# Routing block of an attention and mixture-of-experts kernel: parts of the down products ahead of two waits, and the second early batch's addition moved into the expert block

## What is computed

```python
logits = (x @ wt.T + repeat(g @ wg.T)) / 2
topk_w, topk_idx = top_k(softmax(logits), 2)      # weights normalised to sum 1
y_all = einsum('etm,emh->eth', leaky(x @ w_gate) * (x @ w_up), w_down)
y = (y_all[topk_idx] * topk_w).sum(1)
p = (leaky(x @ sw_gate) * (x @ sw_up)) @ sw_down  # the shared expert
out = x + y + p
```

## Time and profile before

| What | us |
|---|---|
| median of three runs (lowest, highest) | 1751.0 (1750.06, 1754.42) |
| the profiled execution, device time | 1752.34 |
| its span, first to last instruction | 1750.6 |
| PE busy / PEld busy | 1622.9 / 1357.3 |
| DVE / ACT / POOL busy | 972.0 / 719.0 / 730.9 |
| routing block: PE's first matmul to the first of the expert block | 1057.77 to 1158.86 |
| mean granted TensorE clock | 0.969 |

### The profile page before, as it was taken

The page is one execution under the profiler, slowest core; times in us unless marked ns, Lnnn a source line. Parts: engine busy times, 40 slices in busy tenths (PEclk is TensorE's granted clock), DMA queues, the critical chain, the costliest instruction groups (busy, mean ns, idle before and its releaser), DMA issues. The chain is left out here.

```text
span 1750.6 us, 36162 instructions
## 1 busy us (share of the span) xinstructions
PE 1622.9 (93%) x10364; PEld 1357.3 (78%) x10365; DVE 972.0 (56%) x2442; ACT 719.0 (41%) x1823; POOL 730.9 (42%) x1177
## 2 busy tenths in 40 slices
PE   6899987999999999996999997989999999899998
PEld 4777766887888888885888886768777788678886
DVE  5444525776677766775655555624333333356565
ACT  3222325776776766775222221114333343312221
POOL 1000234676676676674655550332222222234222
PEclk9999997999999999998999998989999999999999
DMA  6576657776776766876544452043455533246333
GB/s 214 202 243 227 221 197 219 210 221 187 215 208 187 209 196 180 233 198 160 171 152 159 144 174 78 1 186 108 174 223 216 208 108 106 85 128 221 97 103 114
DMA packets 172361, 301.32 MB, mean 172 GB/s; under 512 B 16658, under 2 KB 64322, under 8 KB 170196
## 3 DMA queue, kind: packets, MB, share of 16 engines
q1 hardware_dynamic: 142324, 235.21, 42.1%
q0 software_dynamic: 11200, 35.73, 7.2%
q10 hardware_dynamic: 18720, 29.12, 4.9%
HBM read 186.99 MB, written 113.00 MB: 171 GB/s over the span
## 5 line engine op out<-in xcount | busy, mean ns | idle before, releaser
L754 POOL TENSOR_SCALAR probs<-probs,rsums 128x512 f32<-128x512 f32 (+3 forms) x512 | 265.1, 536 | 198.6 <-DVE rsums L790 198.5
L782 DVE CUSTOM_DVE_ANT_0 scores<-psum,resident 128x514 f32<-128x514 f32 (+3 forms) x512 | 242.6, 484 | 156.9 <-PE psum L897 136.9
L855 ACT ACTIVATE probs<-scores,lowest 128x514 f32<-128x514 f32 (+3 forms) x512 | 284.3, 557 | 35.0 <-DVE lowest L782 33.8
L909 PE MATMUL psum<-ident,probs 128*128 128x128 f32 x1280 | 234.3, 282 | 19.1 <-DVE probsT L797 13.2
L897 PE MATMUL psum<-keys,queries 128*128 (+4 forms) x640 | 221.2, 354 | 24.0 <-DMA queries_and_ones<-q_hi_d 17.3
L909 PEld LDWEIGHTS psum<-ident,probs 128*128 128x128 f32 x1280 | 150.6, 141 | 53.6 <-issue 39.9
L897 PE MATMUL psum<-keys_lo_and_mask,queries_and_ones 128*128 (+4 forms) x640 | 184.5, 297 | 0.0
L929 PE MATMUL psum<-probsT,v_now 128*64 128x128 f32 x2560 | 169.5, 279 | 0.9 <-DVE probsT L797 0.9
L897 PEld LDWEIGHTS psum<-keys,queries 128*128 128x128 f32 x640 | 126.9, 198 | 34.9 <-issue 20.6
L929 PEld LDWEIGHTS psum<-probsT,v_now 128*64 128x64 f32 x2560 | 138.6, 138 | 14.6 <-issue 1.9
L864 ACT ACTIVATE probsT<-psum 128x512 f32<-128x512 f32 (+2 forms) x192 | 93.6, 488 | 134.5 <-PE psum L909 121.2
(11 more groups left out here) (240 smaller groups left out, 3689.6 us busy)
## 6 DMA issues: line engine op xcount, KB each, us to landing
ys_d<-y_out ACTq DMA_DIRECT2D x71, 256.0 KB
q_hi_d<-q_hi SPq DMA_DIRECT2D x64, 256.0 KB, 2.4
q_lo_d<-q_lo SPq DMA_DIRECT2D x64, 256.0 KB, 2.8
queries<-q_hi_d SPq DMA_DIRECT2D x64, 256.0 KB, 3.7
queries<-q_lo_d SPq DMA_DIRECT2D x64, 256.0 KB, 4.1
queries_and_ones<-q_hi_d SPq DMA_DIRECT2D x64, 256.0 KB, 4.5
oT_d<-o_out SPq DMA_DIRECT2D x64, 256.0 KB, 2.3
o_in<-oT_d SPq DMA_DIRECT2D x32, 512.0 KB, 3.9
```

The lines of the kernel that those rows point to most:

```text
L754: pool.tensor_scalar(out=row, in0=row, scalar1=rsums[:, n % RING:n % RING + 1], scalar2=1.0, op0=ALU.mult, op1=ALU.mult).then_inc(probs_sc ...
L782: dve.tensor_tensor_reduce(out=scores[n % 4][:, 0:CK[i]], in0=score_psum(n), in1=bias_of(resident, i, h), scale=1.0, scalar=3.0e38, op0=AL ...
L855: act.activation(probs[n % RING][:, 0:CK[i]], scores[n % 4][:, 0:CK[i]], ACT.Exp, bias=lowest[:, n % 4:n % 4 + 1], scale=-1.0, accum_out=s ...
L909: last = pe.transpose(probsT_bank[g % 2][:, at + j * P:at + (j + 1) * P], probs[n % RING][:, AHEAD + j * P:AHEAD + (j + 1) * P], ident[:])
```

## The change

`down` gets the chunks that it shall do, and the four `down` of a batch are split in two. `begin_down(b)` waits for the third chunk's `h_lo` and does chunks 0 to 2 of token tiles 0 and 1; `end_down(b)` waits for the fourth, does its three matmuls for both tiles, and then tiles 2 and 3 whole. For batch 0 the one stands right behind the other; for batch 1 `find_tokens(6)` and `find_tokens(7)` stand between them. The additions of x1 to batch 1's tiles leave the routing block: POOL makes two behind the gather of expert tile 2 and two behind that of tile 3, and SP waits for all eight additions before it loads x1 of batch 2 over the buffers.

```diff
+def add_x(pool, partial, x1, b, t, x_added):
+    pool.tensor_tensor(out=partial[:, TB * b + t, :], in0=partial[:, TB * b + t, :], in1=x1[b][:, t, :], op=ALU.add
+                       ).then_inc(x_added, 1)
...
             for t in range(TB):
-                add_x(0, t)
+                pool.wait_ge(y_copied, t + 1)
+                add_x(pool, partial, x1, 0, t, x_added)
...
                 gather_rows(pool, dram, route, ident, spare, s, s, rows, xg, rows_ready, xg_loaded)
-            for t in range(TB):
-                add_x(1, t)
...
-            def down(b, t):
-                if TB * b + t >= 2:
+            def down(b, t, js):
+                if js[0] == 0 and TB * b + t >= 2:
                     pe.wait_ge(y_copied, TB * b + t - 1)
...
-                for j in range(SC):
+                for j in js:
...
-                done.then_inc(y_full, 1)
+                if js[-1] == SC - 1:
+                    done.then_inc(y_full, 1)
+
+            def begin_down(b):
+
+                pe.wait_ge(h_lo_ready, SC * b + SC - 1)
+                for t in range(2):
+                    down(b, t, range(SC - 1))
+
+            def end_down(b):
+                pe.wait_ge(h_lo_ready, SC * b + SC)
+                for t in range(2):
+                    down(b, t, range(SC - 1, SC))
+                for t in range(2, TB):
+                    down(b, t, range(SC))
...
-            pe.wait_ge(h_lo_ready, SC)
-            for t in range(TB):
-                down(0, t)
+            begin_down(0)
+            end_down(0)
...
+            begin_down(1)
             find_tokens(6)
             find_tokens(7)
-            pe.wait_ge(h_lo_ready, 2 * SC)
-            for t in range(TB):
-                down(1, t)
+            end_down(1)
...
                     gather_rows(pool, dram, route, ident, spare, s, k, rows, xg, rows_ready, xg_loaded)
+                    if known(s) and s < 4:
+
+                        for t in range(2 * (s - 2), 2 * (s - 1)):
+                            add_x(pool, partial, x1, 1, t, x_added)
...
+            sp.wait_ge(x_added, EARLY_B * TB)
             for b in range(EARLY_B, EARLY_B + 2):
                 load_x1(sp, dram, x1, b, b % 2, x1_loaded)
```

More of the change, by code:

```diff
@@ L124, in build @@
             xg_loaded = [held.enter_context(nc.semaphore(f"xg_loaded{i}")) for i in range(2)]
+            x_added = held.enter_context(nc.semaphore("x_added"))
             stage_route(nc, dram, psum, ident, logits, shared, route, experts, experts_loaded, x1, x1_loaded, partial,
-                        spare, rows, xg, rows_ready, xg_loaded)
+                        spare, rows, xg, rows_ready, xg_loaded, x_added)
             stage_experts(nc, dram, psum, ident, spare, experts, experts_loaded, route, x1, x1_loaded, rows, xg,
-                          rows_ready, xg_loaded)
+                          rows_ready, xg_loaded, partial, x_added)
         stage_shared(nc, dram, psum, ident, spare, shared, route, x1, x1_loaded, partial, out)
@@ L1240, in stage_route @@
 def stage_route(nc, dram, psum, ident, logits, shared, route, experts, experts_loaded, x1, x1_loaded, partial, spare, rows,
-                xg, rows_ready, xg_loaded):
+                xg, rows_ready, xg_loaded, x_added):
     with ExitStack() as ctx:
@@ L1284, in stage_route @@
                                                     sem("y4_copied"))
-        tokens_ready, x_added = sem("tokens_ready"), sem("x4_added")
+        tokens_ready = sem("tokens_ready")
         at = 2 * EW
@@ L1337, in tile_hots @@
                                    op=ALU.mult).then_inc(tile_hot_ready, 1)
-            def add_x(b, t):
-                pool.wait_ge(y_copied, TB * b + t + 1)
-                pool.tensor_tensor(out=partial[:, TB * b + t, :], in0=partial[:, TB * b + t, :], in1=x1[b][:, t, :], op=ALU.add
-                                   ).then_inc(x_added, 1)
             for t in range(TB):
-                add_x(0, t)
+                pool.wait_ge(y_copied, t + 1)
+                add_x(pool, partial, x1, 0, t, x_added)
             for g in range(GROUPS):
@@ L1624, in _ @@
                     find_tokens(2 * j - 1)
+            begin_down(1)
             find_tokens(6)
             find_tokens(7)
-            pe.wait_ge(h_lo_ready, 2 * SC)
-            for t in range(TB):
-                down(1, t)
+            end_down(1)
 def stage_experts(nc, dram, psum, ident, spare, experts, experts_loaded, route, x1, x1_loaded, rows, xg, rows_ready,
-                  xg_loaded):
+                  xg_loaded, partial, x_added):
     with ExitStack() as ctx:
```

## The result

The changed kernel takes **1739.97 us**, the median of ten runs (1732.28 to 1747.44), against 1751.45 (1743.16 to 1757.08) for ten runs of the kernel before beside it: a ratio of 0.9928, 95% interval 0.9909 to 0.9946, or 12.6 us less by the ratio (9.5 to 15.9). The profiled execution has a span of 1734.8 against 1750.6.

The account below looks back on a forecast made before the run. PE, busy for 93% of the span, was taken to bound the kernel. Batch 0's 5.4 and batch 1's 7.9 sum to 13.3 us off, other terms 0: 1739.0 for the profiled execution, median 1737.7, range 1735.5 to 1743.5.

Parts of the forecast that it names:

- Batch 0: Routing block: 18 matmuls fill PE's wait for `h_lo`, the half clock behind it goes, a bank wait costs 0.2; 5.4 us gained.
- Batch 1's tail: Routing block's end: 18 matmuls fill the 3.42 idle ahead of group 6 and the half clock ends; part of 7.9 us.
- The clock: Batch 1, behind thin matmuls and 0.7 us idle in two pieces: full clock holds, 0 lost; bound 2.4 if it falls.
- the row that held: Profile row of PE where 1.71 us of thin matmuls stood between wide ones and the wide ones kept full steps.
- The first rival: Half clock stays at batch 1: 12 matmuls take 5.26 instead of 2.83, gain 10.9, time 1740.1; chance 0.16.
- Barrier and additions: Routing block's end: ACT's last copy replaces POOL's last addition as the end; leaving the barrier costs 0.52; part of 7.9.
- The moved additions: POOL, expert block: four additions of 1.26 hide behind its waits of 3.67 and 2.50 for PE; cost 0, bound 0.7.
- The bound of 2.5: Expert block's first gathers lose cover; at the slowest gather's 10.7 us they would land 2.5 too late; 0 taken.
- DVE and POOL as the new bound: Rival: DVE and POOL set the pace in the routing block, batch 0's gain is lost, 7.9 left, 1743.1; chance 0.08.
- The slower rival: Expert block: additions hold up gathers, PE waits, never made up; 1756.3 and over; chance 0.04.
- the formula: Slower rival's sum: loss is the four additions' time beyond the pairs' cover of 3.67 and 2.50, 6.2 in all.
- the break-even: Slower rival's threshold: each addition would have to take 6.2 us, losing 18.6, to be slower by over 5.3.

Follow-up runs that it names:

- The first split alone: Against the changed kernel, only batch 0's down products stay split; batch 1 and the additions as before the change: 1749.5 against 1752.7 us, ratio 0.9962.
- the run: Changed kernel with each of the four moved additions followed by three more of the same size on unread data: 1748.12 against 1754.55 us, ratio 0.9974.
- both splits: Changed kernel with batch 1's additions left at the routing block's end: 1741.73 against 1752.7 us, ratio 0.9930; run again unchanged, a single execution of 1742.5.
- four banks: Changed kernel with four PSUM banks for batch 1, so matmuls of tiles 2 and 3 also precede the waits: 1736.72 against 1754.55 us, ratio 0.9896.
- the groups apart: Changed kernel with nine of batch 1's 18 early matmuls ahead of group 6 and nine behind it: single execution, 1744.1 beside a median of 1756.49 us.

## Why the prediction was right, and where a term was off

The time lies inside the range, 2.3 above the forecast by the medians and 1.1 by the ratio. By its steps, in the profiled executions:

- **Batch 0, forecast 5.4, measured 5.4** from the transposes on (17.31 to 11.91; the forecast's sum is 11.9). In the table it is 5.2, as the half clock at the block's start lasted 0.2 longer in this execution. The 18 matmuls end just ahead of `h_lo`; PE goes on 0.06 behind it (DVE ends at 1095.59), as forecast, and the bank costs 0.16 more than a step (forecast 0.2). That the sums agree to a hundredth is in part luck: the 18 began 0.35 behind the transposes' start, not 0.60, then PE stopped 0.12 for `h_lo`, and the first step of the six behind it was a slow one, 0.33. The first split alone gives 5.35 in the table.
- **Batch 1's tail, forecast 6.57 of the 7.9, measured 5.25.** The forecast's last step starts at 1149.40, which makes a tail of 15.53. Executions at the full clock have 15.53 and 15.56. The order of things, both small idles among it, was right: 0.34 for `h_lo`, forecast 0.6.
- **The clock, forecast 0, bound 2.4, measured 1.3.** This is the step that failed: "an idle of 0.7 in pieces is nearer to the first", the row that held. It held in two executions and fell in five of the same order, so neither row decided it. The first rival was the right mechanism at half its price: some nine steps at half clock, not 12. They take 3.64 where the full clock needs 2.04, and some 0.3 of the 1.6 comes back, since the bank is free by then and its stop falls away. The Trainium skill, "TensorE: Matmul & The Clock Gate", Part 1, says that the default state is throttled and activity releases the throttle. The prediction took from it that a PE that is hardly ever idle keeps the full rate; two executions agree with that, and five, with the half clock behind the same idles of 0.28 and 0.34, do not.
- **Barrier and additions, forecast 1.34 of the 7.9, measured 1.56.** ACT is the last, as forecast; leaving the barrier costs 0.30 behind its copy, not 0.52.
- **The moved additions, forecast 0: right.** They take 1.26 each, the lower of the two rows, and leave 1.28 and 0.71 of cover, where 1.1 and nothing were forecast. The first gathers cost nothing either: they land 3.4 behind their issue, and PE's wait at 1146.40 is the barrier's. The bound of 2.5, from gathers beside weight loads, didn't come into it.
- **DVE and POOL as the new bound: refuted** by the first split alone, but with less to spare than forecast. As this rival said, the earlier additions lengthened DVE's work, by 2.1, a term that the forecast put at nothing; DVE's idle shrank to 0.55 instead of 2.6, and PE waited for neither.
- **The slower rival had the right mechanism and the wrong sum.** The excess over the cover of the first pair goes straight into PE's wait, 6.07 against 6.06. But the two pairs do not add: they took 9.88 and 9.79, so the formula would lose 19.7 - 6.2 = 13.5, and the run lost 8.4 to 9.4. "Never made up" held for the first pair alone. By that the break-even would lie above 6.2 each; no run was made there.

## What to carry to other kernels

Where a chain of matmuls waits for its last operand, issue the part that needs only the earlier ones ahead of the wait; its gain can be worked out from the steps between starts, and came out to 0.1 us here where the clock held. Try to fill small idles to the last: 0.6 us left over cost 1.3 more through the clock in five of seven executions, and the two that left none showed no fall. Those two also put wide matmuls between the thin groups, so which of the two things kept the clock up is not separated. Work moved behind another engine's wait was free here while it was shorter than that wait (2.5 of 3.8), and the first piece that was longer cost the waiting engine what it took beyond.

## What was unexpected in the hardware

The same program has the half clock behind two small idles in one execution and not in the next. The two executions of both splits differ earlier, too: at the routing block's start, behind the same 1.41 us of idle, the first keeps the half clock for 14 steps and the second for 10. The timelines of PE, first of the execution without the later fall, where the step goes from 0.43 to 0.24 at 1071.12,

```profile
1064.70 0.80 PE L1573 MATMUL psum<-expert_weights,shared_hi 128*128 128x512 f32 x1 [1.41 <-DVE expert_weights L1514]
...
1071.12 0.40 PE L1573 MATMUL psum<-expert_weights,shared_hi 128*128 128x512 f32 x1
1071.36 0.39 PE L1574 MATMUL psum<-expert_weights,shared_hi 128*128 128x512 f32 x1
```

then of the one with it, where the full step is back at 1072.35, 4.8 us behind the idle instead of 6.4:

```profile
1067.57 0.79 PE L1573 MATMUL psum<-expert_weights,shared_hi 128*128 128x512 f32 x1 [1.41 <-DVE expert_weights L1514]
...
1072.35 0.40 PE L1575 MATMUL psum<-expert_weights,shared_lo 128*128 128x512 f32 x1
```

Over the versions this stretch makes up to 1.5 us between two executions (batch 0 of the table: 37.47 with four banks, 39.02 with the groups apart, for the same instructions), as much as the moved additions gave. The expectation for the second run of both splits foretold the fall from this length (26.72 us from the first gate matmul to the first down matmul, against 27.46), and it came; but with the groups apart the length was 27.42 and the clock fell all the same, behind a longer idle. So the length goes along with the fall in the six executions that have batch 0 split and both small idles, only one of them without the fall, and isn't a rule for it. What fixes the moment at which the clock falls or rises isn't settled by these runs.
